# A fused scan and mixture-of-experts layer on one core: the prologue in another order, the replicated rows in halves, the first drive on VectorE, split output tiles

## The reference

```python
xn = layernorm(x)
# state-space part: D_IN 1024, N 16 states, K 4 taps, R 32
xh, gate = split(xn @ W_in.T)
xh = silu(conv_b + sum_j conv_w[:, j] * xh shifted by K-1-j)
ts, B, C = split(xh @ W_x.T)                  # 32, 16, 16; each through an rms norm
dt = softplus(ts @ W_dt.T + b_dt)
state = state * exp(dt * A) + (dt * xh) * B   # along the 1024 tokens of each row
y = sum_n state * C
s = ((y + xh * D) * silu(gate)) @ W_out.T
# router: 8 experts, the best 2 for each token, softmax of their logits
g = silu(sum_k prob_k * (xn @ expert_w[idx_k]))
out = x + s * g
```

## Time and profile before

| | |
|---|---|
| median of 3 runs | 1232.94 us (1228.55 to 1235.98) |
| the profiled execution | 1238.47 us, span 1236.2 us |
| busy, share of the span | PE 71%, PEld 25%, DVE 88%, ACT 58%, POOL 71% |
| mean granted TensorE clock | 0.834 of full speed |
| chain that ended last | DVE 42%, issue 17%, PE 17%, POOL 9%, DMA 7%, ACT 5% |
| DMA | 219 MB, mean 177 GB/s |

### The profile page before, as it was taken

The page is one execution under the profiler, slowest core; times in us unless marked ns, Lnnn a source line. Parts: engine busy times, 40 slices in busy tenths (PEclk is TensorE's granted clock), DMA queues, the critical chain, the costliest instruction groups (busy, mean ns, idle before and its releaser), DMA issues.

```text
span 1236.2 us, 9959 instructions
## 1 busy us (share of the span) xinstructions
PE 879.8 (71%) x2648; PEld 315.1 (25%) x2648; DVE 1087.6 (88%) x1141; ACT 712.3 (58%) x1250; POOL 876.6 (71%) x333
## 2 busy tenths in 40 slices
PE   4850446888875999888642849688876997887265
PEld 2310111332321333332110313233322332232022
DVE  5663879989979789999999998999979789999992
ACT  2432446667756566777544545677747566666442
POOL 0003788999866988887836837897866998998734
PEclk9975656989887998998775869898978999898668
DMA  9406554766446565654623444564537555665304
GB/s 304 157 3 220 91 118 137 190 207 204 155 187 247 187 244 207 217 209 172 219 68 130 162 139 159 197 246 173 203 144 259 193 213 204 212 216 190 139 21 149
DMA packets 78087, 219.16 MB, mean 177 GB/s; under 512 B 15824, under 2 KB 17232, under 8 KB 71376
## 3 DMA queue, kind: packets, MB, share of 16 engines
q1 hardware_dynamic: 58384, 167.12, 39.9%
q10 hardware_dynamic: 12384, 30.94, 6.3%
q0 software_dynamic: 7264, 20.47, 5.8%
HBM read 176.77 MB, written 41.72 MB: 177 GB/s over the span
## 4 chain that ended last, share of the span: by engine, by line
DVE 42%; issue 17%; PE 17%; POOL 9%; DMA 7%; ACT 5%; SPq 2%; POOLq 0%; DVEq 0%; ACTq 0%
DVE sc_ps L991 19%; DVE drive L991 6%; POOL drive L467 5%; DMA rep<-rep_rows 5%; DVE drive L1001 4%; PE x_ps L1263 4%; PE dt_ps L1191 3%; DVE x_ps L947 2%; PE dt_ps L1159 2%; PE y_ps L1231 2%; PE f_ps L1216 2%; POOL drive L480 1%; ACT sc_ps L649 1%; DVE dt_ps L970 1%; DVE dt_ps L972 1%
## 5 line engine op out<-in xcount | busy, mean ns | idle before, releaser
L467 POOL TENSOR_TENSOR drive<-rep,b_all 128x2048 f32<-128x2048 f32 x128 | 580.7, 4541 | 243.7 <-DMA rep<-rep_rows 185.5
L649 ACT ACTIVATE sc_ps<-rep,a_neg 128x512 f32<-128x512 f32 x512 | 332.5, 682 | 173.4 <-DVE drive L1001 118.9
L1231 PE MATMUL y_ps<-drive,stack 128*32 128x512 f32 x1024 | 169.0, 740 | 152.7 <-DVE drive L1001 115.8
L991 DVE TENSOR_TENSOR_SCAN sc_ps<-sc_ps,drive 128x512 f32<-128x512 f32 x184 | 214.7, 1212 | 46.9 <-POOL drive L467 30.1
L991 DVE TENSOR_TENSOR_SCAN sc_ps<-sc_ps,state,drive 128x512 f32<-128x512 f32 x184 | 225.7, 1272 | 19.1 <-ACT sc_ps L649 19.1
L1001 DVE TENSOR_TENSOR drive<-sc_ps,c_all 128x1024 f32<-128x1024 f32 x184 | 225.3, 1225 | 6.3
L480 POOL TENSOR_TENSOR drive<-drive,c_all 128x1024 f32<-128x1024 f32 x72 | 170.0, 2361 | 20.2 <-ACT state L628 17.9
L1191 PE MATMUL dt_ps<-xnT,w_g 128*128 128x512 f32 x232 | 138.4, 751 | 60.9 <-ACT dtu L616 60.9
L1216 PE MATMUL f_ps<-w_ring,xT_slot 128*128 128x512 f32 x368 | 169.1, 602 | 5.7 <-ACT xT_slot L661 5.7
L1139 PE MATMUL x_ps<-xnT,w_x 128*128 128x512 f32 x192 | 97.6, 655 | 6.5 <-DMA w_x<-wx_in 6.5
L1216 PEld LDWEIGHTS f_ps<-w_ring,xT_slot 128*128 128x128 f32 x368 | 69.3, 194 | 105.0 <-issue 105.0
(11 more groups left out here) (153 smaller groups left out, 1036.1 us busy)
## 6 DMA issues: line engine op xcount, KB each, us to landing
rep<-rep_rows SPq DMA_DIRECT2D x128, 512.0 KB, 6.5
w_ring<-wring SPq DMA_DIRECT2D x46, 1024.0 KB, 6.2
rep_rows<-dtu ACTq DMA_DIRECT2D x32, 512.0 KB, 2.9
slot_rows<-y_slot ACTq DMA_DIRECT2D x46, 256.0 KB, 3.3
w_g<-wg_in SPq DMA_DIRECT2D x32, 256.0 KB, 2.7
w_x<-wx_in SPq DMA_DIRECT2D x24, 256.0 KB, 4.3
rep<-x SPq DMA_DIRECT2D x16, 256.0 KB, 5.5
xn_rows<-rep SPq DMA_DIRECT2D x16, 256.0 KB, 3.0
```

The costliest lines, as they stand in the source:

```text
L467: pool.tensor_tensor(drive[:, m % RING, :, :], rep[:, n % 2, :, 1, :], b_all[:, q:q + 1, :].broadcast_to([P, NR, TC]), ALU.mult).then_inc( ...
L649: act.activation(sc[:, r, :], rep[:, n % 2, r, 0, :], ACT.Exp, scale=a_neg[:, lo:lo + 1]).then_inc(decay_ok, 1)
L991: dve.tensor_tensor_scan(to, sc[:, r, :], drive[:, m % RING, r, :], state[:, lo:lo + 1] if follows else 0.0, ALU.mult, ALU.add).then_inc(s ...
L1231: last = pe.matmul(y_ps[CH * r:CH * (r + 1), :], stack[:, :], drive[:, m % RING, r, :], start=False, stop=(m % NQ == NQ - 1))
```

## The change

The edits are all of them in the order of work or in the place of a buffer.

- Loads: x tiles 0 and 1 of chunk 0 are issued by SyncE, 2 and 3 by ScalarE ahead of its table load, each with a semaphore of its own, and VectorE takes each tile's statistics when that tile is there.
- ScalarE copies the first four transposes ahead of its wait for the constants.
- Three PSUM banks and three pads (two of them in slots 2 and 3 of `drive`) hold the input of chunk 0's convolutions, so that projection t waits for convolution t - 3 only.
- VectorE: statistics and normalising of the other 12 tiles are cut into pieces that stand between the convolutions. The router's ranks and rows go behind the convolutions.
- TensorE: the transposes of tiles 4 to 15 go behind the last projections, the router logits behind `step_sizes(0)`.
- ScalarE: the copy of the logits and `keep_rows(0)` stand ahead of `softplus(1)`; both pairs of decays of quad 0 are made before the loop.
- `rep` is waited for in halves (rows 0 and 1, rows 2 and 3) by ScalarE, and by VectorE for quad 0.
- Drive 0 is made by VectorE in two halves of 128x1024, each just ahead of its scans; `route_rows` stands between the two halves, `route_ranks` ahead of `step_sizes(1)`, and that ahead of the first drive. GpSimd no longer waits for `slot_ok` before drive 1.
- `w_out` is loaded at tile 3.
- The scatters: row 0's are spread over quads 1 to 3 of tile 0 and quad 0 of tile 1 (6, 4, 4 and 2), row 1's over tiles 2 to 5 (two in quads 0 and 2 of each).
- At the last tile of the even chunks (k = 7) the low product of quad 2 goes from GpSimd to VectorE.
- Output tiles 0 and 2 of an even chunk are cut in two, four pairs of matmuls ahead of `sums(m + 1)` and four behind it.

```diff
-POOL_QUADS = {k: (0, 1, 2) if 1 < k < 14 else () for k in range(16)}
+POOL_QUADS = {k: (0, 1) if k == NT - 1 else (0, 1, 2) for k in range(2, 14)}
...
         def x_bank(j):
-            return sc[:, 2, :] if j < NT and j % 2 else x_ps[:, :]
+            return (x_ps[:, :], sc[:, 2, :], sc[:, 3, :])[j % 3] if j < NT else x_ps[:, :]
...
         @block.sync
-            for i in range(TT):
-                sp.dma_start(x_in[:, i, :], x_t[i]).then_inc(s_x[0], 16)
+            for i in range(TT // 2):
+                sp.dma_start(x_in[:, i, :], x_t[i]).then_inc(s_x0[i], 16)
...
                     sp.dma_start(rep[:, k % 2, r, :, :].rearrange("p k t -> p (k t)"),
-                                 rows.broadcast_to([CH, NG, 2 * TC])).then_inc(s_rep[k % 2], 16)
+                                 rows.broadcast_to([CH, NG, 2 * TC])).then_inc(s_rep[k % 2][r // 2], 16)
...
-            for half in range(2):
-                sp.dma_start(w_out[:, HK * half:HK * (half + 1), :], wring[E + half]).then_inc(s_wo, 16)
...
+                if n == 3:
+                    for half in range(2):
+                        sp.dma_start(w_out[:, HK * half:HK * (half + 1), :], wring[E + half]).then_inc(s_wo, 16)
...
         @block.gpsimd
+            def puts_at(n, q):
+                if n == 0:
+                    return 0, (0, 0, 3, 5)[q], (0, 3, 5, 7)[q]
+                if n == 1 and q == 0:
+                    return 0, RT - 1, RT
+                if 2 <= n < 6 and q in (0, 2):
+                    return 1, 2 * (n - 2) + q // 2, 2 * (n - 2) + q // 2 + 1
+                return 0, 0, 0
...
-            pool.wait_ge(slot_ok, 1)
-            pool.wait_ge(s_const, 16 * 9)
-            pool.wait_ge(s_zero, 16 * BATCH)
-            pool.wait_ge(x_mm, NT)
-            drives(0)
+            pool.wait_ge(conv_ok, NT)
             drives(1)
...
                 if n == 0:
-                    put_in_order(0, 4, RT)
-                if 1 <= n <= 4:
-                    put_in_order(1, 2 * n - 1, 2 * n)
+                    pool.wait_ge(slot_ok, 1)
+                    pool.wait_ge(s_const, 16 * 9)
+                    pool.wait_ge(s_zero, 16 * BATCH)
+                put_in_order(*puts_at(n, 1))
                 drives(NQ * n + 4)
                 low_products(NQ * n + 2)
+                put_in_order(*puts_at(n, 2))
...
         @block.scalar
+            for i in range(TT // 2, TT):
+                act.dma_start(x_in[:, i, :], x_t[i]).then_inc(s_x0[i], 16)
...
             def copy_x(j):
-                if j:
-                    act.wait_ge(conv_ok, j)
-                    act.wait_ge(halo_ok, j)
+                kept = j - 2 if j < NT else j
+                if kept > 0:
+                    act.wait_ge(conv_ok, kept)
+                    act.wait_ge(halo_ok, kept)
...
+            copy_transposed(range(TT))
             act.wait_ge(s_const, 16 * 9)
             act.activation(a_neg[:, :], a_neg[:, :], ACT.Exp).then_inc(a_exp, 1)
-            copy_transposed(range(TT))
-            copy_x(0)
+            for t in range(3):
+                copy_x(t)
...
+            for t in range(3, NT):
                 copy_x(t)
+                if t == NT - 1:
+                    copy_transposed(range(TT, 6))
+                silu_x(t - 1)
+            copy_transposed(range(6, 10))
+            silu_x(NT - 1)
...
             rms(0)
+            act.preload_act_table_set(LNEXP)
             rms_root(0)
+            copy_transposed(range(10, 16))
             softplus(0)
             keep_dt(0)
+            act.wait_ge(lgT_mm, 1)
+            act.copy(logit_T[:, :], f_ps[:, :]).then_inc(lgT_ok, 1)
+            keep_rows(0)
             softplus(1)
-            keep_rows(0)
             act.wait_ge(a_ok, 1)
             decays(0, 0)
+            decays(0, 1)
+            act.wait_ge(lg_d, 1)
+            act.activation(logit[:, :, :], logit[:, :, :], ACT.Exp).then_inc(lg_e, 1)
...
         @block.vector
+            spreads(1)
+            dve.wait_ge(a_exp, 1)
+            dve.tensor_scalar(a_neg[:, :], a_neg[:, :], -1.0, None, ALU.mult).then_inc(a_ok, 1)
+            spreads(2)
+            convolve(0)
+            spreads(3)
+            variances(TT, NCH * TT)
+            convolve(1)
+            roots(2, TT, NCH * TT)
             dve.wait_ge(dve_link, links[0])
-            for j in range(3):
-                convolve(j)
-            route_ranks(0, E // 2)
+            convolve(2)
+            normalise(range(TT, 2 * TT))
             convolve(3)
-            route_ranks(E // 2, E)
-            for j in range(4, NT):
-                convolve(j)
-            route_rows()
+            normalise(range(2 * TT, 3 * TT))
+            convolve(4)
+            normalise(range(3 * TT, 4 * TT))
+            for t in range(5, NT):
+                convolve(t)
...
             rms(0)
             step_sizes(0)
+            route_ranks(0, E)
+            step_sizes(1)
+            dve.wait_ge(s_b[0], 16)
+            dve.wait_ge(conv_ok, NT)
+            for h in range(2):
+                dve.wait_ge(s_rep[0][h], REP // 2)
+                dve.tensor_tensor(drive[:, 0, 2 * h:2 * h + 2, :], rep[:, 0, 2 * h:2 * h + 2, 1, :],
+                                  b_all[:, 0:1, :].broadcast_to([P, 2, TC]), ALU.mult).then_inc(first_ok, 1)
+                scans(0, h)
+                products(0, h)
+                if h == 0:
+                    route_rows()
             route_weights()
...
         @block.tensor
             for t in range(NT):
-                if t == 1:
-                    project_x(t, lambda h: x_w[:, t, P * h:P * (h + 1)])
-                    transposes(range(TT, NCH * TT))
-                    pe.wait_ge(tr_ev, NCH * TT)
-                    add_ssm(0, 0)
-                    router_logits()
-                    continue
-                if t >= 2:
-                    pe.wait_ge(conv_ok, t - 1)
+                if t >= 3:
+                    pe.wait_ge(conv_ok, t - 2)
                 project_x(t, lambda h: x_w[:, t, P * h:P * (h + 1)])
-                if t:
-                    add_ssm(0, t - 1)
-                if t == 2:
-                    turn_logits()
-            count_pairs()
+                if t >= 4:
+                    add_ssm(0, t - 4)
+            for t in range(NT - 4, NT - 2):
+                add_ssm(0, t)
+            transposes(range(TT, 6))
+            add_ssm(0, NT - 2)
+            transposes(range(6, 10))
             add_ssm(0, NT - 1)
             means_of(0)
+            transposes(range(10, 16))
             step_sizes(0)
+            pe.wait_ge(tr_ev, NCH * TT)
+            router_logits()
+            turn_logits()
             step_sizes(1)
+            count_pairs()
...
                 if not even and t in (0, 1):
-                    out_tile(c - 1, 2 * t)
+                    out_tile(c - 1, 2 * t, 0, HK)
                 if late is not None:
                     next_x(NT * (c + 1) + late)
                 turn_slot(b, second_slot)
                 sums(m + 1)
+                if not even and t in (0, 1):
+                    out_tile(c - 1, 2 * t, HK, NT)
```

More of the change, by code:

```diff
@@ L164, in xn_part @@
             return xnT[:, c, h, :] if c < 2 else later_xnT[:, c - 2, h, :]
+        first_ok = sem("first_ok")
         s_const = sem("s_const")
+        s_x0 = [sem(f"s_x0_{i}") for i in range(TT)]
         s_x = [sem(f"s_x{g}") for g in range(NCH)]
@@ L175, in scan_moe @@
         s_c = [sem(f"s_c{q}") for q in range(NQ)]
-        s_rep = [sem(f"s_rep{a}") for a in range(2)]
+        s_rep = [[sem(f"s_rep{a}_{h}") for h in range(2)] for a in range(2)]
         s_wo = sem("s_wo")
@@ L1058, in _ @@
                 after_odd, after_even = c and even, not even
-                low(m)
-                if n == 0:
-                    step_sizes(1)
-                high(m)
+                if n:
+                    low(m)
+                    high(m)
                 if n:
@@ L1131, in count_pairs @@
                 for k, m in enumerate((before, ones)):
[L1132 removed]
+                    last = pe.matmul(f_ps[:, P * k:P * (k + 1)], m, both[:, :, :].rearrange("p t e -> p (t e)"),
                                      start=True, stop=True)
```

105 lines of the change are left out of this document (53 added, 52 removed).

## The result

The changed kernel took 1219.72 us (median of 4 runs, 1216.22 to 1221.26) beside 1232.73 for the kernel before (4 runs). The ratio is 0.9892, with an interval from 0.9855 to 0.993: faster by about 1%, 13.0 us where 26.5 were forecast. 1219.72 lies in the range, but near its slow end. The profiled execution took 1221.26 us, span 1218.7, against 1238.47 and 1236.2.

The account below looks back on a forecast made before the run. VectorE, busy 1087.6 of 1236 us, was taken as the bound. Tile 1 22.5 plus borders 6 minus tiles 2 to 5's 2 gave 26.5 us, median 1232.9 to 1206.4 us; range 1195 to 1221.

Parts of the forecast that it names:

- The start of the chain: Prologue: statistics, projections and convolutions come earlier, so `rep_rows` is written at 75.8 instead of 101.2, 25.4 us earlier.
- the hold: Tile 0: GpSimd's drives 1 to 3 block VectorE's small two-SBUF-input operations in `route_rows`; cost 7.7 us, from 0 to 9.
- the halves of `rep`: Before tile 0's first scan: give VectorE next to nothing, since the second half is there when it is ready.
- No hold: Rival in tile 0: VectorE's small operations slip between GpSimd's drives, the 7.7 us stay saved: 1198 us; chance 0.12.
- TensorE at its lower level: Rival in the prologue: TensorE stays at 1.2 GHz, costing 34 us against 26.5 gained: 1240 us; chance 0.04.
- it does nothing: Rival: the time is bound elsewhere and the prologue's gain becomes idle time: 1233 us; chance 0.05.
- The first tiles give back: Rival: `w_out` and its scatters delay `rep(4)` and expert inputs by 10 us instead of 2: 1215 us; chance 0.17.
- the stall, "11.7": Start of tile 1: VectorE's wait from 151.3 to 163.0 for late copies of `rep` goes, saving 11.7 us.
- tiles 2 to 5, 2 us lost: Tiles 2 to 5: `w_out` meets expert loads and a gather, tile 5 has extra scatters; 2 us lost, between 0 and 10.
- the borders, "6 us": Two chunk borders: the low product moved to VectorE ends TensorE's wait for GpSimd; 3 us each, 6 us, between -2 and 10.
- counted at 0, hidden in the same 6: Borders: the split output tile changes only the order, one `sums` going 3.5 us sooner in 4 tiles; counted at 0.
- tile 1 22.5: Tile 1's start at 140.5 instead of 163.0, summing the prologue's gains less the costs on VectorE: 22.5 us earlier.

Follow-up runs that it names:

- the changed kernel's second trace: The changed kernel profiled again with no edit; 1218.84 us against 1235.88 for the kernel before (17 runs), ratio 0.987.
- all three comparisons: The changed kernel, unedited, timed three times against the kernel before: ratios 0.9892, 0.987 and 0.9892.

## Why the forecast was too large

**What was right.** The start of the chain and its order. The statistics ended at 7.52 instead of 9.98, 2.5 us sooner (2.2 forecast). The rule of the Trainium skill (DMA: Bandwidth & Descriptors, section Issuing engines are not separate DMA queues) that a second issuing engine saves only its sequencer's time would have given 1; but each tile also had a wait of its own here, and no run parts the two, so it is neither borne out nor refuted. Projection 0 began at 14.71 (15.0), the convolutions ended at 51.5 (52.9), `rep_rows` was issued 29.3 earlier (25.4), although it took 5.9 us to land where 2.6 were seen before. First scan at 84.8 (88.3), drive half on VectorE 1.22 us (1.22). GpSimd's first drive began at 86.51, when the second half of `rep` was there (ScalarE's decays of it began at 86.30). The Trainium skill (SBUF — State Buffer, section SBUF: two separate sides) would have let VectorE's half drive hold it, but that had ended at 84.80, so the two never met and this direction of the lock was not tested. In the other direction the trace agrees with it: the hold was forecast at 7.7 us and `route_rows` lasted 9.1 us longer, two single operations lasting 4.4 us beside drives of 4.5. Tile 1's stall went; landing of `rep(1)` in the changed kernel's second trace, SyncE's issues from 85 to 120 us:

```profile
DMA to landing us min/median/max: 6.5/6.9/7.2
```

That is under the 10 us forecast, against 12.1 to 25.5. Tile 1 came at 138.3 (140.5).

Two things in this part came out by other numbers than the prediction's. It says that the halves of `rep` give VectorE next to nothing. VectorE was ready at 83.66, the first half had come by 83.1 and the second by 86.3, so they let the first scan run 2.7 us sooner; but VectorE was then held until GpSimd's drives ended at 99.95, and GpSimd starts with the second half, so little of the 2.7 us can have been left. And its own numbers give a hold of 6.9, not 7.7: three drives of 13.5 us from 87.3 end at 100.8, not 102, and of 9.9 us less 2 there are 7.9 left, not 7.5.

**The rivals.** *No hold* is refuted by 9.93 us for seven operations, *TensorE at its lower level* by the clock of 1.00 up to 70 us, *it does nothing* by all three comparisons. *The first tiles give back* is what happened in part; its time, 1215, is the nearest to the 1219.7 measured, but of the 13.5 us that are missing only 5.3 are its own.

**First failed step: the stall, "11.7".** It was read in one profiled execution. Two more traces of the kernel before start tile 1 at 157.1 and 158.0, so about 5.5 of the 11.7 us belonged to that execution (3.6 of them against the mean of all three). The sum was made against the execution (1238.5) and then taken off the median (1232.9) whole, with a stall in it that the median run does not have: an execution 5.5 us above the median was said to be so, but not asked where the 5.5 us were. Against the mean of three traces tile 1 gained 20.8, not 22.5: the chain of the changed kernel ran 2.0 us faster than forecast (138.5 against 140.5), and that hides part of the error.

**Second: "tiles 2 to 5, 2 us lost".** They lost 7.3 (131.0 to 138.3). The mechanism was named, `w_out`'s 2 MB beside gathers and expert loads, and the size was wrong. Tile 3 lost 3.7 us: its first gather took 9.5 to 10.3 us to land, TensorE waited 7.3 to 8.1 for it, ScalarE's decays stood behind that, and VectorE waited 6.8 to 7.1 us in all for ScalarE. With `w_out` at tile 1 that gather landed in 6.5 us and the four tiles lasted 131.9. Tile 2 lost 2.4 us to a slower gather before the load was issued, and tile 4 lost 5.1 us in one trace of three, behind the write of `rep_rows`, which took 12.2 to 13.3 us instead of 3.1 to 3.8. No row of the sum stood for the gather of tile 2 or for the write.

**Third: the borders, "6 us".** They brought 0.8. Two terms are in it. The quad's move is worth 4.9 us where 6 were forecast, by the run without it. And the split, "counted at 0, hidden in the same 6", cost 2.5 by the run without it. The two would leave 2.4 and 0.8 was measured; tiles 7 to 10 alone differ by 1.8 us between traces of the changed kernel, so the rest stays open. The gate projection did start 6.0 us earlier against the tile, but the gather ended its gain, and with that taken away TensorE waited for VectorE's gating (1.85 us) and for GpSimd's low product (2.10 us).

As a sum, forecast against the mean of three traces: tile 1 22.5 against 20.8; tiles 2 to 5, 2 against 7.3 lost; borders 6 against 0.8; all other tiles 0 against 1.4 lost. 26.5 against 12.9.

## What to carry to other kernels

Before a stall of a single profiled execution becomes a term of a sum, look whether that execution lies off the median, and take a second trace: a wait on copies that share their time with scatters is not the same twice. When a large load is moved, look for the small transfers that the next work waits for and that go out behind it, whatever engine issues them: here a gather by GpSimd, and a write by ScalarE. And a chain of small VectorE operations with both inputs in SBUF belongs ahead of GpSimd's large ones, not beside them, even if GpSimd starts later for it.

## What the runs showed that was not expected

- The chain of small operations is held longer than each operation would be alone: seven of them waited for two whole drives (9.93 us, against 1.43 with GpSimd idle). The next drive starts 0.1 us ahead of the next small operation (95.46 and 95.56), and that one waits for it too. The profile books the wait as busy time of VectorE.
- The same four copies of 512 KB of the same kernel, beside the same scatters, released GpSimd at 158.4, 152.6 and 153.5 us in three executions.
- A write of 512 KB issued by ScalarE 4 us behind 3 MB that SyncE had issued (`w_out` and an expert's weights) took 13.3, 12.9 and 12.2 us in three traces; in three of the kernel before it took 3.7, 3.1 and 3.8.
